# Cross-attention and FFN kernel: attention weights transposed in row halves, a head at a time

## What is computed

```python
# x: 32 x 256 x 256; 16 heads of 64; keys and values from side (256 rows) and from ctx (256 rows)
xn  = layernorm(x)
k   = concat(side @ Wk.T + bk, ctx @ Wgk.T + bgk)      # 512 keys
v   = concat(side @ Wv.T + bv, ctx @ Wgv.T + bgv)
q   = xn @ Wq.T + bq
att = q k^T / 8, -inf where mask, for the first 256 keys only
x   = x + (softmax(att) v) @ Wo.T + bo
x   = x + ffn(layernorm(x))                             # fp8-quantised 256 x 256 product, bf16 bias
```

## Time and profile before

| | |
|---|---|
| median of 3 runs | 2607.75 us (2606.32 to 2608.06) |
| profiled execution, its own time | 2607.76 us |
| its span | 2606.0 us |
| PE (TensorE products) busy | 2571.1 us, 20352 instructions |
| PEld (weight loads) busy | 2357.9 us |
| DVE busy | 2147.9 us |
| POOL busy | 2058.9 us |
| ACT busy | 1858.1 us |
| transposes, L870 | 4096, busy 557.8 us, 275 ns each |

### The profile page before, as it was taken

How to read it: one execution, slowest core, us unless ns; L and a number is a source line. 1 busy time by engine, 2 the same in 40 slices (tenths; PEclk the granted TensorE clock), 3 DMA queues, 4 the chain that set the end, 5 groups by cost and what they waited for, 6 DMA issues and landing times.

```text
span 2606.0 us, 67610 instructions
## 1 busy us (share of the span) xinstructions
PE 2571.1 (99%) x20352; PEld 2357.9 (90%) x20352; DVE 2147.9 (82%) x5344; ACT 1858.1 (71%) x4464; POOL 2058.9 (79%) x2499
## 2 busy tenths in 40 slices
PE   7999999999999999999999999999999999999997
PEld 6899999999999999999999999999999999999996
DVE  7888888888878888888888888887888888888877
ACT  6776677777677766777667777767776677777775
POOL 6787777887778877778777788877887777887775
PEclk9999999999999999999999999999999999999999
DMA  5000100101000001000010010100001100101000
GB/s 159 17 23 26 32 24 24 32 16 32 28 28 24 16 32 32 24 24 24 25 32 25 24 32 16 32 28 28 24 16 32 32 24 24 31 18 32 28 17 13
DMA packets 59983, 75.19 MB, mean 29 GB/s; under 512 B 5168, under 2 KB 42032, under 8 KB 59952
## 3 DMA queue, kind: packets, MB, share of 16 engines
q1 hardware_dynamic: 59952, 74.81, 9.3%
HBM read 66.40 MB, written 8.39 MB: 29 GB/s over the span
## 4 chain that ended last, share of the span: by engine, by line
PE 97%; DVE 1%; issue 0%; SPq 0%; DMA 0%; ACT 0%; POOL 0%; POOLq 0%; DVEq 0%; ACTq 0%
PE ps_work L742 35%; PE ps_o L885 19%; PE ps_pt L870 18%; PE ps_work L858 15%; PE ps_work L819 8%; PE ps_work L828 1%; PE ps_work L798 1%; DVE probs L1517 0%; PE ps_work L824 0%; DMA wo_sb<-wq_t_dram 0%; DVE pt_lo L1528 0%; PE ps_work L787 0%; DVE wgv_lo L1548 0%; SPq L380 0%; SPq L387 0%
## 5 line engine op out<-in xcount | busy, mean ns | idle before, releaser
L549 POOL TENSOR_SCALAR probs<-probs,recips 128x512 f32<-128x512 f32 x1024 | 717.4, 714 | 197.5 <-DVE recips L1524 197.4
L1528 DVE TENSOR_TENSOR pt_lo<-ps_pt,pt_hi 128x512 fp32r<-128x512 f32 x1024 | 671.8, 682 | 159.7 <-ACT pt_hi L1149 155.3
L1142 ACT ACTIVATE probs<-probs,neg_max 128x512 f32<-128x512 f32 x1024 | 734.7, 722 | 62.8 <-DVE neg_max L1517 60.9
L1149 ACT CAST pt_hi<-ps_pt 128x512 fp32r<-128x512 f32 x1024 | 561.0, 591 | 302.4 <-PE ps_pt L870 291.1
L1517 DVE CUSTOM_DVE_ANT_1 probs<-ps_work,mask_sb 128x512 f32<-128x512 f32 x960 | 618.8, 683 | 69.7 <-PE ps_work L858 66.6
L870 PE MATMUL ps_pt<-ident,probs 128*128 128x128 f32 x4096 | 557.8, 275 | 3.6 <-DVE pt_lo L1528 1.7
L885 PE MATMUL ps_o<-pt_hi,v_hl 128*128 128x256 f32 x2048 | 537.2, 295 | 0.6 <-DVE pt_lo L1528 0.6
L870 PEld LDWEIGHTS ps_pt<-ident,probs 128*128 128x128 f32 x4096 | 455.9, 141 | 71.7 <-issue 52.3
L885 PE MATMUL ps_o<-pt_lo,v_hl 128*128 128x256 f32 x2048 | 508.0, 281 | 0.0
L885 PEld LDWEIGHTS ps_o<-pt_hi,v_hl 128*128 128x128 f32 x2048 | 386.5, 189 | 35.4 <-issue 34.2
L885 PEld LDWEIGHTS ps_o<-pt_lo,v_hl 128*128 128x128 f32 x2048 | 388.2, 190 | 0.1
(11 more groups left out here) (125 smaller groups left out, 5928.1 us busy)
## 6 DMA issues: line engine op xcount, KB each, us to landing
mask_sb<-mask_dram SPq DMA_DIRECT2D x128, 256.0 KB, 3.4
x_sb<-x_dram SPq DMA_DIRECT2D x32, 256.0 KB, 2.7
side_raw<-side_t_dram SPq DMA_DIRECT2D x32, 256.0 KB, 3.7
scr_b<-ctx_t_dram SPq DMA_DIRECT2D x32, 256.0 KB, 2.7
out_dram<-y SPq DMA_DIRECT2D x31, 256.0 KB, 2.1
wo_sb<-wo_t_dram SPq DMA_DIRECT2D x1, 1024.0 KB, 5.5
v_bias<-bv_dram SPq DMA_DIRECT2D x1, 512.0 KB, 6.3
v_bias<-bgv_dram SPq DMA_DIRECT2D x1, 512.0 KB, 7.1
```

The costliest lines, as they stand in the source:

```text
L549: nc.gpsimd.tensor_scalar(p, p, recips[:, h % RING, t:t + 1], 1.0, ALU.mult, ALU.mult).then_inc(norm_done, 1)
L1142: nc.scalar.activation(p, p, ACT.Exp, bias=neg_max[:, h % RING, t:t + 1], scale=-1.0, accum_out=sums[:, h % RING, t:t + 1]).then_inc(exp_d ...
L1149: nc.scalar.copy(pt_hi[:, h % 2, 2 * k:2 * k + 2, :], ps_pt[:, k, :, :]).then_inc(pthi_done, 1)
L1528: V.tensor_tensor(pt_lo[:, h % 2, 2 * k:2 * k + 2, :], ps_pt[:, k, :, :], pt_hi[:, h % 2, 2 * k:2 * k + 2, :].bitcast(F32), ALU.subtract). ...
```

## The change

The transposes of a head are now made in one call of 16, `transposes(c, h)`. Each takes the 64 queries of one row half (partitions 0 to 63, or 64 to 127) and one key tile: 64 rows by 128 columns as weights, and a 64x64 piece of the identity streamed. The two halves alternate, half e writes bank e of `ps_pt`, so a bank now holds all four key tiles of half of the queries. The last of the 16 raises `pt_full` by 2, and the first waits for `norm_done` and for both `pt_lo` of the head before, each in a semaphore instruction of its own (`wait_apart`). `pt_his` and `pt_los` copy one bank each as before, now scattered over `pt_hi` and `pt_lo` in runs of 64. The lists of ACT, DVE and POOL are unchanged. On TensorE each head's two calls become one, which stands where the second stood if there was anything between them.

```diff
-        ps_pt = psum("ps_pt", [P, 2, 2, S])
+        ps_pt = psum("ps_pt", [P, 2, KT, P])
...
+        def half_queries(pt, h, e):
+
+            return pt[:, h % 2, :, :].rearrange("p k (t e q) -> p k t e q", t=QT, e=2)[:, :, :, e, :]
...
-            def transposes(c, h, k):
-                if k == 0:
-                    pe.wait_ge(norm_done, QT * c.head(h) + QT)
+            def transposes(c, h):
+
+                wait_apart(pe, "pe", norm_done, QT * c.head(h) + QT)
                 if some(c.head(h)):
-                    pe.wait_ge(ptlo_done, 2 * c.head(h) - 1 + k)
-                for j in range(2):
-                    for t in range(QT):
-                        kt = 2 * k + j
-                        last = nc.tensor.transpose(ps_pt[:, k, j, t * P:(t + 1) * P],
-                                                   probs[:, h % RING, t, kt * P:(kt + 1) * P], ident[:])
-                last.then_inc(pt_full, 1)
+                    wait_apart(pe, "pe", ptlo_done, 2 * c.head(h))
+                for t in range(QT):
+                    for kt in range(KT):
+                        for e in range(2):
+                            own = slice(e * DK, (e + 1) * DK)
+                            last = nc.tensor.transpose(ps_pt[:, e, kt, t * DK:(t + 1) * DK],
+                                                       probs[own, h % RING, t, kt * P:(kt + 1) * P], ident[own, own])
+                last.then_inc(pt_full, 2)
...
-                transposes(c, 2, 0)
                 scores(c, 4, 0, after=(("wo0_prev", 0), None))
                 scores(c, 4, 1, after=(("q", 1), ("k1", 1)))
-                transposes(c, 2, 1)
+                transposes(c, 2)
...
-                transposes(c, 4, 0)
                 outputs(c, 3)
-                transposes(c, 4, 1)
+                transposes(c, 4)
...
-                nc.scalar.copy(pt_hi[:, h % 2, 2 * k:2 * k + 2, :], ps_pt[:, k, :, :]).then_inc(pthi_done, 1)
+                nc.scalar.copy(half_queries(pt_hi, h, k), ps_pt[:, k, :, :].rearrange("p k (t q) -> p k t q", t=QT)
+                               ).then_inc(pthi_done, 1)
...
-                V.tensor_tensor(pt_lo[:, h % 2, 2 * k:2 * k + 2, :], ps_pt[:, k, :, :],
-                                pt_hi[:, h % 2, 2 * k:2 * k + 2, :].bitcast(F32), ALU.subtract).then_inc(ptlo_done, 1)
+                V.tensor_tensor(half_queries(pt_lo, h, k), ps_pt[:, k, :, :].rearrange("p k (t q) -> p k t q", t=QT),
+                                half_queries(pt_hi, h, k).bitcast(F32), ALU.subtract).then_inc(ptlo_done, 1)
```

More of the change, by code:

```diff
@@ L901, in _ @@
             scores(f, 2, 1, after=(None, None))
-            transposes(f, 0, 0)
-            transposes(f, 0, 1)
+            transposes(f, 0)
             chunk(f, "k0", 1, after=(2, 0))
@@ L906, in _ @@
             chunk(f, "k1", 1, after=(2, 1))
-            transposes(f, 1, 0)
-            transposes(f, 1, 1)
+            transposes(f, 1)
             outputs(f, 0)
@@ L911, in _ @@
             scores(f, 4, 1, after=(("q", 1), ("k1", 1)))
-            transposes(f, 2, 0)
             chunk(f, "v0", 1, after=(4, 0))
-            transposes(f, 2, 1)
+            transposes(f, 2)
             chunk(f, "q", 2, after=(4, 1))
             outputs(f, 1)
-            transposes(f, 3, 0)
-            transposes(f, 3, 1)
+            transposes(f, 3)
             outputs(f, 2)
@@ L923, in _ @@
             chunk(f, "v1", 1, after=(6, 0))
-            transposes(f, 4, 0)
-            transposes(f, 4, 1)
+            transposes(f, 4)
             outputs(f, 3)
@@ L928, in _ @@
             chunk(f, "k1", 2, after=(6, 1))
-            transposes(f, 5, 0)
-            transposes(f, 5, 1)
+            transposes(f, 5)
             scores(f, 8, 0, after=(("v1", 1), ("v0", 2)))
@@ L936, in _ @@
             chunk(f, "k0", 3, after=(8, 1))
-            transposes(f, 6, 0)
             outputs(f, 5)
-            transposes(f, 6, 1)
+            transposes(f, 6)
             chunk(f, "k1", 3, after=(8, 1))
-            transposes(f, 7, 0)
-            transposes(f, 7, 1)
+            transposes(f, 7)
             scores(f, 10, 0, after=(("xq_prev", 0), ("q", 3)))
@@ L976, in _ @@
             scores(f, 16, 1, after=(("k1", 0), ("v1", 3)))
-            transposes(f, 14, 0)
-            transposes(f, 14, 1)
+            transposes(f, 14)
             chunk(f, "v1", 0, after=(16, 0))
             outputs(f, 13)
-            transposes(f, 15, 0)
-            transposes(f, 15, 1)
+            transposes(f, 15)
             outputs(f, 14)
@@ L987, in batch @@
                 scores(c, 2, 1, after=(None, None))
-                transposes(c, 0, 0)
-                transposes(c, 0, 1)
+                transposes(c, 0)
                 outputs(c, -1)
@@ L1005, in batch @@
                 outputs(c, 1)
-                transposes(c, 3, 0)
-                transposes(c, 3, 1)
+                transposes(c, 3)
                 chunk(c, "k0", 2, after=(4, 1))
@@ L1017, in batch @@
                 chunk(c, "k1", 2, after=(6, 1))
-                transposes(c, 5, 0)
-                transposes(c, 5, 1)
+                transposes(c, 5)
                 scores(c, 8, 0, after=(("v1", 1), ("v0", 2)))
@@ L1022, in batch @@
                 outputs(c, 4)
-                transposes(c, 6, 0)
-                transposes(c, 6, 1)
+                transposes(c, 6)
                 chunk(c, "v1", 2, after=(8, 0))
-                transposes(c, 7, 0)
                 chunk(c, "q", 3, after=(8, 0))
@@ L1029, in batch @@
                 outputs(c, 5)
-                transposes(c, 7, 1)
+                transposes(c, 7)
                 chunk(c, "xq_prev", 0, after=(8, 0))
@@ L1046, in batch @@
                 chunk(c, "zt_next", 0, after=(12, 0))
-                transposes(c, 10, 0)
-                transposes(c, 10, 1)
+                transposes(c, 10)
                 chunk(c, "ff_prev", 0, after=(12, 0))
@@ L1051, in batch @@
                 chunk(c, "q", 0, after=(12, 1))
-                transposes(c, 11, 0)
-                transposes(c, 11, 1)
+                transposes(c, 11)
                 outputs(c, 10)
@@ L1056, in batch @@
                 scores(c, 14, 1, after=(("q", 0), ("v1", 3)))
-                transposes(c, 12, 0)
-                transposes(c, 12, 1)
+                transposes(c, 12)
                 outputs(c, 11)
@@ L1061, in batch @@
                 chunk(c, "v0", 0, after=(14, 0))
-                transposes(c, 13, 0)
-                transposes(c, 13, 1)
+                transposes(c, 13)
                 chunk(c, "k1", 0, after=(14, 1))
@@ L1068, in batch @@
                 scores(c, 16, 1, after=(("k1", 0), ("v1", 3)))
-                transposes(c, 14, 0)
-                transposes(c, 14, 1)
+                transposes(c, 14)
                 last_attended(c, 1, range(0, 5))
@@ L1073, in batch @@
                 chunk(c, "v1", 0, after=(16, 0))
-                transposes(c, 15, 0)
-                transposes(c, 15, 1)
+                transposes(c, 15)
                 outputs(c, 14)
```

29 lines of the change are left out of this document (10 added, 19 removed).

## The result

The changed kernel takes 2763.31 us (median of 5 runs, 2762.54 to 2777.72) against 2607.69 for the kernel before (median of 5): ratio 1.0611, 95% interval 1.0597 to 1.0624. It is 156 us slower. (The profiled execution, 2777.72 us, is the longest of the five.) I had forecast 2611 in a range of 2575 to 2650, so the prediction was wrong, and by far more than its sum could move.

A forecast was written before the change was run, and what follows sets the result against it. TensorE was taken to set the time. Its 2.6 us a round gain, against held places, summed to -0.11, and +0.20 for start latency made +0.09: +3 us in 31 rounds on 2607.76, 2611 us, range 2575 to 2650.

The forecast's parts named there:

- The two added semaphore instructions per head: TensorE's queue, before each head's transposes (T): cost nothing where T is not waiting, 0.05 us where it is.
- the slower one: Rival: half-height loads take 0.11 or halves do not overlap, so a pair costs 0.109 us; 2716 us, chance 0.12.
- p: Time of one pair of half transposes on TensorE: between 0.055 and 0.11 us, taken as 0.060.
- Gain on the array: TensorE alone, 16 heads' transposes: ten gain 0.05 us each, six beside scores about 0.35, together 2.6 us a round.
- lone heads: Ten heads whose transposes (T1, T3 and others) stand between full-array work: 0.87 us becomes 0.82, a gain of 0.05 each.
- Held places: Places where TensorE waits for other engines after whole-head release, such as scores 4, T6, T9, T12: 2.7 us a round.
- T14's gain: Transposes of head 14: their gain goes whole, because outputs(13) waits for DVE's addition; 0 in the round's sum.
- Round: One loop round, gains and holds summed: -0.11 us, with +0.20 for longer start latency +0.09; round 80.1 to 80.3 us.
- The span of 2591 to 2643: Whole kernel's us, for p between 0.055 and 0.075 and held places good to 0.3 us a round in sum.
- Outside the loop: First batch taken as nearly the same order as the loop's 30 rounds, so 31 rounds counted at +0.09 us each.
- Copies: pt_hi and pt_lo copies, now in runs of 64: no longer than before (591 and 682 ns), at most 0.05 us apiece.
- TensorE is not held: Rival: slack at T6 and T9 is made up as other queues move up; 2527 us, or 2567 if half; chance 0.15.

The follow-up runs named there:

- first_5_full: The changed kernel with transposes of all 128 rows for heads 0 to 4 of batch 0, ahead of the loop; loop body unchanged: 2626.01 us.

## Why the prediction was wrong

**The step that failed.** The sum counted time on the array, and of what the change adds to the queue it said: "The two added semaphore instructions per head run ahead of the array: nothing where T is not waiting". They are 16 of the 272 instructions that a round gains, net of waits that it drops; 256 are the loads and products of the half transposes. Nothing in the working asked what a longer loop body costs. It costs 137 us of the 156 (2763.31 less 2626.01, first_5_full): 3.1 us at each turn, and the clock at half for 4.6 us a round. The trace of before held the clue, had I looked: one packet in the queue "instruction" inside the loop, in its second round, and 1421 instructions over seven blocks already. Neither rival had this mechanism: the slower one had its price from the array too.

**The rest, by its steps.** In first_5_full, where nothing is fetched anew, the change costs 18.5 us (ratio 1.0071, 1.0056 to 1.0087) against my +3.

- *p*: forecast 0.060 a pair. A block of 16 takes 0.43 to 0.49 us from first to last start; its pairs are 0.060 to 0.065 apart, and where the first load is not hidden the first step is 0.11. That is right, near the edge: the sum called itself measurably slower above 0.061. The rival of 0.109 fell, and with it, for these transposes, the rule of the Trainium skill ("TensorE: Matmul & The Clock Gate", LDWEIGHTS) that 128 columns take 128 / 1.2 ns whatever the rows.
- *Gain on the array*: forecast 2.6 us a round, measured 80.09 less 78.23, 1.9. From the product ahead of a block to the second one behind it, lone heads (T3) went from 1.11 to 1.08, 0.03 for the 0.05 forecast; T5, ahead of scores, from 1.42 to 1.02, 0.40 for 0.35; T0, behind scores, from 1.37 to 1.20, 0.17 for 0.35, with its first product 0.10 later behind the scores than T14's. But the busy time counts the end of the last product before a wait, up to 0.28 us, as work: at T6 0.96 of idle time stand for 1.02 between starts. By starts the waits come to some 2.8 us a round and the gain to some 2.5, an estimate from the distances in the next item; so the sum was nearer than the busy time says.
- *Held places*: forecast 2.7, by busy time 2.2 (80.39 less 78.23), by starts some 2.8: 1.0 at T6 (0.8 forecast), 0.3 at T9 (0.4), 0.5 at T12 (0.2), 0.2 at scores 4 (0.4), and 0.4 at zt_next, 0.4 at outputs(13) and 0.1 at T0. At the last three I had none, and gave T14's gain whole. The waits of the round:

```profile
PE ps_pt L890 <- POOL probs L561: 1.0, 1, 1.0
PE ps_pt L890 <- DVE pt_lo L1524: 0.5, 2, 0.3
PE ps_o L905 <- DVE o_t L1534: 0.3, 1, 0.3
PE ps_work L810 <- DVE neg_max L1509: 0.2, 1, 0.2
```

- *Round*: forecast +0.09, measured +0.30, or 8.8 us over 29 periods. It came out near because misses at single places, up to 0.4 us and of both signs, nearly cancel; that is luck. (The span of 2591 to 2643 took the 0.3 of the held places off its lower end and did not add it to the upper, which would be 2653.)
- *Outside the loop*: I counted 31 rounds alike. The loop's first turn comes 6.5 us later than before, and the part behind the last one is 2.5 longer. The first batch has its own order, and I had not read it.
- *Copies*: unchanged at 591 and 683 ns, as forecast.

*"TensorE is not held"* is out: the array waits for over 2 us of each round.

## What to carry to other kernels

Count an engine's instructions in a loop body, before and after, as a cost of its own: splitting products in two doubles their number, however little time it takes on the array. When the profile's queue of instructions carries packets inside a loop, or "issue" stands ahead of a round's first product, look at how many blocks of 256 the body touches and how much room it leaves at the end; a few instructions more or fewer ahead of the loop may be worth more than any edit in it. And where other engines run at 80% behind a full TensorE, array time saved at one place is taken back at the next hold, so split a change by places and keep only those that keep their gain, as heads 0, 5 and 14 did here with 0.27 us of their 0.95.

## What the hardware did that I had not expected

- A loop of 1693 TensorE instructions runs from the buffer or is fetched whole at each turn, 9 packets of 16 KB, depending on its start alone: 2626 to 2639 us or 2763 to 2854.
- Bodies over seven blocks stayed and bodies over eight did not, and with 27 instructions of room at the end of the seventh block it depended on the order of the work near the turn: 0, 10 or 29 turns of 29 were fetched.
- A stall of some 3 us at the turn went with the clock at 0.50 for 3.4 or 6.8 us at 28 of 29 turns.
- Semaphore increments on TensorE's queue cost 6 ns each at 144 a round and 27 ns each at 272, both spread over the same products.
